# Attention steps spread over more half-slots, transposes of P earlier in SyncE's queue, one rotation product instead of two

## The reference

```
x = x + 0.5 * ffn(layernorm(x))
x = x + attn(layernorm(x))
x = x + 0.5 * ffn(layernorm(x))        # the same FFN weights again

ffn:  p = softmax(x @ router.T)        # 8 experts
      w = p where the cumulated sorted p stays within 0.9 (the first over it kept), else 0
      out = sum_e w[:, e] * ((silu(x @ gate_e.T) * (x @ up_e.T)) @ down_e.T)      # inner width 512
attn: q (16 heads of 16), k and v (4 heads of 16); bias; RMS norm and rotation of q and k; q * gain
      softmax(q k^T / 4 + causal mask) @ v, then @ Wo.T + bo
```

## Time and profile before

| | |
|---|---|
| median of three runs | 1158.7 us |
| the profiled execution | 1158.12 us |
| its span | 1156.4 us |
| TensorE busy | 1098.6 us, 95% |
| VectorE, ScalarE, GpSimd busy | 72%, 47%, 54% |
| mean DMA throughput | 48 GB/s |
| mean granted TensorE clock | 0.996 |

### The profile page before, as it was taken

One profiled execution on the slowest core, in us unless ns is written; L12 is line 12 of the kernel. 1 busy time (PEld: TensorE's weight loads), 2 busy tenths in 40 slices (PEclk: granted clock), 3 DMA queues, 4 the chain that ended last, 5 costly groups with the idle time before them and its releaser, 6 DMA issues.

```text
span 1156.4 us, 21016 instructions
## 1 busy us (share of the span) xinstructions
PE 1098.6 (95%) x7553; PEld 658.0 (57%) x7553; DVE 834.8 (72%) x1817; ACT 544.0 (47%) x1026; POOL 629.5 (54%) x657
## 2 busy tenths in 40 slices
PE   5899999998998998998998999999999999999998
PEld 2465555664564654664665655655655556556565
DVE  7878887666877877887887788787788765544443
ACT  4545544333644544654654555555555553333332
POOL 4544443446567557567567578577487453322322
PEclk9999999999999999999999999999999999999999
DMA  5411210000323223233232232333323321000000
GB/s 183 131 55 56 73 50 2 11 14 19 52 51 65 51 41 65 51 52 56 51 52 56 51 52 56 56 65 69 60 42 70 59 51 20 5 19 1 1 2 19
DMA packets 157303, 55.86 MB, mean 48 GB/s; under 512 B 149392, under 2 KB 154000, under 8 KB 157200
## 3 DMA queue, kind: packets, MB, share of 16 engines
q1 hardware_dynamic: 157200, 54.51, 22.4%
HBM read 15.70 MB, written 2.10 MB: 15 GB/s over the span
## 4 chain that ended last, share of the span: by engine, by line
PE 55%; POOL 8%; issue 3%; DMA 3%; DVE 2%; SPq 1%; ACT 1%; DVEq 0%; POOLq 0%; ACTq 0%
PE YB L338 18%; PE G L319 16%; PE U L319 16%; DMA QKT<-room 3%; POOL RR L1032 2%; POOL HS L976 2%; PE S L442 1%; PE S L428 1%; POOL room L1058 1%; PE S L411 1%; SPq L1155 1%; POOL XF L989 1%; PE S L393 1%; POOL RA L1027 1%; DVE X L627 1%
## 5 line engine op out<-in xcount | busy, mean ns | idle before, releaser
L976 POOL TENSOR_TENSOR HS<-TS,HS 128x512 f16<-128x512 f32 x256 | 301.3, 1177 | 402.6 <-ACT HS L491 402.0
L338 PE MATMUL YB<-W,HS 128*128 128x256 f16 x3036 | 377.3, 274 | 20.8 <-DVE X L627 16.9
L319 PE MATMUL G<-XS,W 128*128 128x512 f16 x1536 | 376.3, 381 | 1.7 <-ACT XS L516 1.7
L319 PE MATMUL U<-XS,W 128*128 128x512 f16 x1536 | 373.7, 379 | 1.0 <-DVE W L712 1.0
L338 PEld LDWEIGHTS YB<-W,HS 128*128 128x128 f16 x3036 | 289.9, 98 | 95.1 <-DVE X L627 25.5
L491 ACT ACTIVATE HS<-TS 128x512 f16<-128x512 f32 x256 | 161.3, 630 | 337.9 <-DVE TS L611 336.0
L606 DVE SCALAR_TENSOR_TENSOR TS<-TS,G 128x512 f32<-128x512 f32 x256 | 174.9, 683 | 191.0 <-ACT TS L484 190.7
L484 ACT ACTIVATE TS<-G,TSC 128x512 f32<-128x512 f32 x256 | 175.5, 685 | 180.9 <-PE G L319 176.8
L319 PEld LDWEIGHTS U<-XS,W 128*128 128x128 f16 x1536 | 150.3, 98 | 182.9 <-DVE W L712 1.5
L319 PEld LDWEIGHTS G<-XS,W 128*128 128x128 f16 x1536 | 150.0, 98 | 130.8 <-issue 2.6
L611 DVE SCALAR_TENSOR_TENSOR TS<-TS,U 128x512 f32<-128x512 f32 x256 | 176.0, 687 | 28.4 <-DVE TS L606 1.8
(11 more groups left out here) (160 smaller groups left out, 748.5 us busy)
## 6 DMA issues: line engine op xcount, KB each, us to landing
room<-in_gate SPq DMA_DIRECT2D x4, 512.0 KB, 3.5
room<-in_up SPq DMA_DIRECT2D x4, 512.0 KB, 3.4
room<-in_down SPq DMA_DIRECT2D x4, 512.0 KB, 4.3
QKT<-in_gate SPq DMA_DIRECT2D x4, 512.0 KB, 3.5
QKT<-in_up SPq DMA_DIRECT2D x4, 512.0 KB, 4.0
QKT<-in_down SPq DMA_DIRECT2D x4, 512.0 KB, 4.7
out_y<-X SPq DMA_DIRECT2D x16, 128.0 KB, 1.8
X<-in_x SPq DMA_DIRECT2D x3, 512.0 KB, 6.1
```

The source lines that it names most:

```text
L319: mm = eng.matmul(bank[:, :], W[:, e, wl, jj, kk * I + m * P:kk * I + (m + 1) * P], flat(XS16[:, b % 2, xl, kk, :, :], 'cq'), start=q == 0 ...
L338: mm = eng.matmul(out, HS[:, j % 2, hl, kk, m * P:(m + 1) * P], W[:, e, wl, 2, kk * D:(kk + 1) * D], start=kk + hl + wl == 0, stop=kk == K ...
L976: eng.tensor_tensor(HS[:, j % 2, 1, m, :], TS[:, k % 3, :], HS[:, j % 2, 0, m, :], ALU.subtract).then_inc(L['g_lo'].sem, 1)
```

## The change

Only places in the queues, one wait list and one VectorE product change. All shapes, matmuls and DMAs stay. Rounds 3 and 4 of a batch move from r = 20 and 26 to 18 and 27 (the others stay), the projection moves one slot later, so does most of what follows it; even and odd tiles' rounds get offsets of their own.

```diff
-ROUND = [FIRST + 2 + PER * i for i in range(NR)]
+ROUND_AT = (2, 8, 14, 18, 27, 32)
+ROUND = [FIRST + BATCH * (i // PER) + ROUND_AT[i % PER] for i in range(NR)]
...
-FTP_SOON, FTP_LATER, FTP_LAST, ROUTE_LATER = ((66, 68), (62, 64), (30, 51), 67)
+FTP_SOON, FTP_LATER, FTP_LAST, ROUTE_LATER = ((64, 64), (61, 62), (32, 49), 67)
...
-A_STEP = {'ax': 3, 'xl': 3, 'bo': 6}
-Q_STEP = {'rb1': 2, 'sq': 2, 'rb0': 2, 'rr': 3, 'r': 4, 'qn': 5, 'v': 5, 'qh': 6, 'ql': 6, 't': 7}
-I_STEP = {'ma': 1, 'mb': 2, 'ea': 2, 'eb': 3, 'ha': 3, 'hb': 4, 'la': 4, 'lb': 5, 't': 6, 'pv': 8, 'o': 9}
-R_STEP = {'r1': 1, 'ex': 1, 'r2': 1, 'r2b': 3, 'rank': 3, 'r3': 5}
+A_STEP = {'xn': 2, 'ax': 3, 'xl': 4, 't': 2, 'bo': 7}
+Q_STEP = {'qb': 1, 'rb': 1, 'sq': 1, 'ra': 2, 'ss': 2, 'rr': 4, 'r': 5, 'qn': 5, 'v': 7, 'qh': 6, 'ql': 7, 't': 6}
+EVEN_STEP = {'ma': 1, 'mb': 2, 'ea': 3, 'eb': 3, 'ha': 5, 'hb': 5, 'la': 4, 'lb': 4, 't': 2, 'pv': 8, 'o': 9}
+ODD_STEP = {'ma': 1, 'mb': 2, 'ea': 2, 'eb': 3, 'ha': 2, 'hb': 5, 'la': 3, 'lb': 4, 't': 3, 'pv': 8, 'o': 9}
+AT = {c: [ROUND[i] + (EVEN_STEP if i % PER < 2 else ODD_STEP)[c] for i in range(NR)] for c in EVEN_STEP}
+R_STEP = {'r1': 1, 'ex': 2, 'r2': 2, 'r2b': 3, 'rank': 4, 'r3': 5}
...
-O_STEP = {'ot': 2, 'mm': 2, 'ad': 3}
+O_STEP = {'ot': 1, 'mm': 2, 'ad': 3}
...
-ATP, QKVP, OUTP = (by_tile(-17, -5), by_tile(-12, 0), by_tile(18, 42))
-ATT = [s - 4 for s in ATP]
+ATT, QKVP, OUTP = (by_tile(-24, -12), by_tile(-11, 1), by_tile(18, 42))
...
-TILE = [s - 4 - (f % 2 == 0 and f >= 3 * BT) for f, s in enumerate(FTP)]
+TILE_AT = (-5, -4)
+TILE = [s + (TILE_AT[f % 2] if f >= NT else -4) - (f % 2 == 0 and f >= 3 * BT) for f, s in enumerate(FTP)]
...
-        def dve_rb(eng, t, a):
+        def dve_rb(eng, t):
...
-            eng.tensor_tensor(RB[:, :, a, :], q4[:, :, 1 - a, :], (SIN, NSIN)[a][:, t % 2, :].unsqueeze(1).broadcast_to([P, QK, HD // 2]), ALU.mult).then_inc(L['v_rb'].sem, 1)
+            eng.tensor_tensor(RB[:, :, :, :], q4[:, :, ::-1, :], SIGN[:, t % 2, :, :].unsqueeze(1).broadcast_to([P, QK, 2, HD // 2]), ALU.mult).then_inc(L['v_rb'].sem, 1)
...
         def sp_slot(eng, s):
-            for i in due(ROUND, s, I_STEP['t']):
+            for i in due(AT['t'], s):
                 sp_pt(eng, i)
-            for t in due(ATP, s):
+            for t in due(ATT, s, A_STEP['t']):
                 sp_atp(eng, t)
```

More of the change, by code:

```diff
@@ L169, in build @@
         GM, GE, GR, NESC = (sb(c, [P, 1], F32) for c in ('GM', 'GE', 'GR', 'NESC'))
-        COS, SIN, NSIN = (sb(c, [P, 2, HD // 2], F32) for c in ('COS', 'SIN', 'NSIN'))
+        COS, SIN = (sb(c, [P, 2, HD // 2], F32) for c in ('COS', 'SIN'))
+        SIGN = sb('SIGN', [P, 2, 2, HD // 2], F32)
         ident = sb('ident', [P, P], F32)
@@ L217, in build @@
                 ('v_fst', 'stats'), ('v_fag', 'aggr'), ('v_fep', 'eps'), ('v_fx', 'xn'), ('v_ls', 'ls mx sub'), ('v_rp', 'sum rc p eq gt'), ('v_wt', 'cum wt'), ('v_wb', 'wtc'), ('v_wc', 'wc'),
-                ('v_al', 'stats aggr eps'), ('v_ax', 'xn'), ('v_qb', 'qb'), ('v_ss', 'ss ms'), ('v_rb', 'rb1 rb0 r'), ('v_qn', 'qn'), ('v_ql', 'qlo klo'), ('v_mp', 'xa a xb b'), ('v_pv', 'rc rd ob'), ('v_op', 'ad'),
+                ('v_al', 'stats aggr eps'), ('v_ax', 'xn'), ('v_qb', 'qb'), ('v_ss', 'ss ms'), ('v_rb', 'rb r'), ('v_qn', 'qn'), ('v_ql', 'qlo klo'), ('v_mp', 'xa a xb b'), ('v_pv', 'rc rd ob'), ('v_op', 'ad'),
                 ('g_lo', 'lo'), ('g_w', 'lo2'), ('g_frs', 'rs'), ('g_fl', 'xl'), ('g_rk', 'eq b bp'), ('g_ars', 'rs'), ('g_al', 'xl'), ('g_bo', 'bo'), ('g_sq', 'sq'), ('g_rr', 'rr sg'), ('g_ra', 'ra'), ('g_v', 'v1 r1 v2 r2 v3'), ('g_pl', 'a b'), ('g_rw', 'b1 r1 b2 r2 b3')]:
@@ L297, in s2_read @@
         def s2_read(eng, s):
-            eng.wait_ge(*L['v_pv'].at(before(ROUND, s, I_STEP['pv']), 'rd'))
+            eng.wait_ge(*L['v_pv'].at(before(AT['pv'], s), 'rd'))
             eng.wait_ge(*L['v_qb'].at(before(QKVP, s), 'qb'))
@@ L459, in pe_slot @@
                 pe_scores(eng, i, s)
-            for i in due(ROUND, s, I_STEP['pv']):
+            for i in due(AT['pv'], s):
                 pe_pv(eng, i, s)
@@ L586, in act_slot @@
             for h in range(2):
-                for i in due(ROUND, s, I_STEP['e' + 'ab'[h]]):
+                for i in due(AT['e' + 'ab'[h]], s):
                     act_exp(eng, i, h)
             for h in range(2):
-                for i in due(ROUND, s, I_STEP['h' + 'ab'[h]]):
+                for i in due(AT['h' + 'ab'[h]], s):
                     act_ph(eng, i, h)
@@ L812, in dve_ss @@
             eng.tensor_scalar(MS[:, :], SS[:, :], 1.0 / HD, RMS_EPS, ALU.mult, ALU.add).then_inc(L['v_ss'].sem, 1)
-        def dve_rb(eng, t, a):
+        def dve_rb(eng, t):
             eng.wait_ge(*L['v_qb'].at(t, 'qb'))
             q4 = QKV[:, 0:QW].rearrange('p (h a c) -> p h a c', a=2, c=HD // 2)
-            eng.tensor_tensor(RB[:, :, a, :], q4[:, :, 1 - a, :], (SIN, NSIN)[a][:, t % 2, :].unsqueeze(1).broadcast_to([P, QK, HD // 2]), ALU.mult).then_inc(L['v_rb'].sem, 1)
+            eng.tensor_tensor(RB[:, :, :, :], q4[:, :, ::-1, :], SIGN[:, t % 2, :, :].unsqueeze(1).broadcast_to([P, QK, 2, HD // 2]), ALU.mult).then_inc(L['v_rb'].sem, 1)
         def dve_r(eng, t):
-            eng.wait_ge(*L['v_rb'].at(t, 'rb0'))
+            eng.wait_ge(*L['v_rb'].at(t, 'rb'))
             eng.wait_ge(*L['g_ra'].at(t, 'ra'))
@@ L846, in dve_max @@
                 eng.wait_ge(s_i2, 2)
-                eng.wait_ge(s_ag, 7)
+                eng.wait_ge(s_ag, 8)
             if t % 2 == 0:
@@ L880, in dve_constants @@
             eng.tensor_reduce(GM[:, :], GN[:, :], AX.X, ALU.max, apply_absolute_value=True).then_inc(lane, 1)
-            eng.tensor_scalar(NSIN[:, :, :], SIN[:, :, :], -1.0, None, ALU.mult).then_inc(lane, 1)
-            eng.wait_ge(lane, 2)
+            eng.tensor_scalar(SIGN[:, :, 0, :], SIN[:, :, :], 1.0, None, ALU.mult).then_inc(lane, 1)
+            eng.tensor_scalar(SIGN[:, :, 1, :], SIN[:, :, :], -1.0, None, ALU.mult).then_inc(lane, 1)
+            eng.wait_ge(lane, 3)
             eng.tensor_scalar(GM[:, :], GM[:, :], 1e-30, None, ALU.max).then_inc(lane, 1)
-            eng.wait_ge(lane, 3)
+            eng.wait_ge(lane, 4)
             eng.tensor_scalar(GE[:, :].bitcast(I32), GM[:, :].bitcast(I32), 2139095040, None, ALU.bitwise_and).then_inc(lane, 1)
-            eng.wait_ge(lane, 4)
+            eng.wait_ge(lane, 5)
             eng.reciprocal(GR[:, :], GE[:, :]).then_inc(lane, 1)
             eng.tensor_scalar(NESC[:, :], GE[:, :], -(float(HD) ** (-0.5)), None, ALU.mult).then_inc(lane, 1)
-            eng.wait_ge(lane, 6)
+            eng.wait_ge(lane, 7)
             eng.tensor_scalar(GF[:, :], GN[:, :], GR[:, 0:1], None, ALU.mult).then_inc(lane, 1)
@@ L901, in dve_slot @@
             for h in range(2):
-                for i in due(ROUND, s, I_STEP['m' + 'ab'[h]]):
+                for i in due(AT['m' + 'ab'[h]], s):
                     dve_max(eng, i, h)
-            for i in due(ROUND, s, I_STEP['o']):
+            for i in due(AT['o'], s):
                 dve_pv(eng, i)
-            for t in due(QKVP, s, 1):
+            for t in due(QKVP, s, Q_STEP['qb']):
                 dve_qb(eng, t)
@@ L911, in dve_slot @@
                 dve_a_stats(eng, t)
-            for t in due(ATT, s, 1):
+            for t in due(ATT, s, A_STEP['xn']):
                 dve_a_xn(eng, t)
[L914 to L917, removed]
+            for t in due(QKVP, s, Q_STEP['rb']):
+                dve_rb(eng, t)
+            for t in due(QKVP, s, Q_STEP['ss']):
                 dve_ss(eng, t)
@@ L1023, in pool_ra @@
         def pool_ra(eng, t):
+            eng.wait_ge(*L['v_qb'].at(t, 'qb'))
             eng.wait_ge(*L['v_qn'].at(t - 1, 'qn'))
@@ L1085, in pool_slot @@
             for h in range(2):
-                for i in due(ROUND, s, I_STEP['l' + 'ab'[h]]):
+                for i in due(AT['l' + 'ab'[h]], s):
                     pool_pl(eng, i, h)
@@ L1089, in pool_slot @@
                 pool_sq(eng, t)
+            for t in due(QKVP, s, Q_STEP['ra']):
                 pool_ra(eng, t)
```

## The result

The changed kernel takes 1116.9 us (median of four runs, 1116.35 to 1117.56) against 1158.8: a ratio of 0.9637, 95% interval 0.9623 to 0.9651. That is 41.9 us less; I had forecast 31 less, with a lower end of 1118. The direction and the places were right, the size was not, and the experiments show that two of my steps were wrong in a way that the total hides. Where a difference to the changed kernel is given as a range, it is against 1117.6 and against 1116.9.

What follows compares the result with a forecast made beforehand. TensorE, busy for 95% of the span, was taken as the bound: 17.0 (P) + 12 (X) + 3.2 (lo) + 5.1 (clock) won, 6 given back, net 31.3 off 1158.1, so 1127 us, range 1118 to 1143.

Steps and rivals of the forecast that it cites:

- The residue of 6 us: Waits on TensorE expected to stay or come: 4 us for round 4's P, 2 us for lo.
- the reachable sum: Most the change could win on TensorE: 34.2 us of waits plus 5.1 us of lower clock, 39.3 us.
- all of X: Waits of y for VectorE's add into X: 14.0 us reachable, 12 taken as gone, bounds 8 and 14.
- the rest of the moves at zero: `ot`, `bo`, router steps, `pool_ra`, FFN tiles: work moved within engines' idle time, zero, bounds 2 lost and 1 won.
- all 17.0 us before the product with V: TensorE's waits for P's transposes, put down to queueing on SyncE: 17.0 us won by placing P ahead.
- 3.2 for lo: TensorE's waits for GpSimd's lo: 3.2 us, to go with the late y.
- three stretches of 3.4 us at the lower clock: TensorE at half speed behind waits of 2.7 us or more: 5.1 us won, bounds 0 and 5.1.
- the lo of r = 34: On GpSimd behind round 4's low part and V's parts: 0.5 us late in four batches, 2 us, bounds 0 and 8.
- its own bounds: Whole forecast with residues 0 to 16 and X 8 to 14: 1120 to 1138 us.
- The queue explains the wait to the last tenth.: Round 4's P: SyncE issues its transpose 1.84 us after the low parts end; TensorE waited 1.83 us.
- GpSimd's lack of room: Rival: GpSimd's queue has 13.0 us of work in 12.0; 12 to 18 us more given back, 1141 us, chance 0.15.
- All of it goes: Rival: `qn` on VectorE isn't blocked by a lo, the 6 us don't come; 1119 to 1121 us, chance 0.12.

Runs made afterwards that it cites:

- a_rest_old: Changed kernel with the steps of the router, the second FFN's layernorm and transposes, and `ot` back where they were: 1124.9 us.
- b_both: Kernel before with P's transposes sooner in SyncE's queue and `qn` behind the add into X, none of the other moves: 1146.0 us.
- b_qn_later: Kernel before with only `qn` moved behind the add into X of its slot: 1168.9 us, ratio 1.009.
- b_p_v_qn: Kernel before with P's transposes sooner, V's parts two slots later on GpSimd and `qn` behind the add into X: 1133.6 us, ratio 0.978.

## Why the prediction was right and wrong

Two steps of the prediction failed. The residue of 6 us was a mis-sized term: no such wait came. And the reachable sum itself, 39.3 us, was too small, since it took each wait from the end of a TensorE row: 23 waits were longer than listed, by 3.7 us together. Even without any residue and with all of X my sum ends at 1118.8, above the 1116.4 of the profiled run. A third step, the rest of the moves at zero, was wrong too, but it is no separate term of the waits: what these moves bring was counted among the waits for X and lo.

*Which waits go.* Right: all 17.0 us before the product with V, 11.4 of those for X (I took 12), 3.2 for lo, and three stretches of 3.4 us at the lower clock, 5.1 us.

*The residue (4 + 2 us).* Wrong, the largest single part of the miss. For P the working gave a slack of 0.5 to 1.4 us, and I priced 0.5 us of wait all the same; the batch shown has 0.9, and no batch waits. A reckoned slack above nothing was charged as a cost. The 2 us were for the lo of r = 34, reckoned 0.5 us late. That count began at the worst end of the low parts, T + 3.2, took V's parts at 2.0 us and had them done at T + 7.1. In the trace the low parts end at T + 2.4, V's parts take 1.6 us and are done at T + 5.8, and this lo ends 1.0 us before it is wanted.

*The length of a wait.* Too short by about 0.16 us each. Before, the U ahead of round 4's product has six matmuls that start 0.216 us apart, 1.30 in all, while its row shows 1.46:

```profile
784.88 1.46 PE L319 MATMUL U<-XS,W 128*128 128x512 f16 x6
```

The row's end is modelled, and the listed wait counts only from there. The product could have started at 784.88 + 1.30 = 786.18; it lost 1.99 us, not 1.83. In the changed kernel, without a wait, the product starts 1.31 us after a y whose row shows 1.47. The listed waits for X, P and lo went from 30 to 7; over 23 of them this is 3.7 us, and it is most of why steady batches fell below what I had read. The Trainium skill says it too, in Perfetto Trace Analysis (section Tensor Engine Instruction): the end is an estimate worked out from the instruction's size and an SBUF delay. The rows here agree. I had even added the 0.16 into TensorE's being ready.

*The start.* G of chunk 16 starts at 85.5 us in the changed kernel's profile and at 87.3 before. 0.4 of these 1.8 us is the y that waits for X at 53 us, 1.3 in place of 1.7; it follows the routers' steps, since `a_rest_old` has 1.7 again, and is part of the 11.4. The other 1.4 us lie ahead of it and differ from run to run: this G starts between 85.5 and 87.1 in the traces of the changed kernel and its variants with the new routers' steps. That part is no effect of the change.

With the measured sizes the sum closes on the 41.8 us between the two profiled spans: 31.3 + 6 (residue) - 0.6 (X) + 3.7 (ends) + 1.4 (start) = 41.8.

One sum of the prediction is off as well: its own bounds, taken together, give 1118.8 to 1140.8, not 1120 to 1138.

*"The queue explains the wait to the last tenth."* True of one batch and wrong as a cause. The order alone leaves 5.3 us of waits for P; in the steady batch shown TensorE had itself been held for 1.7 us at y, and without that hold P would have been late by GpSimd's queue (`b_both` waits 2.0 us there). The waits at y and at P are links of one chain from the 3.5 us power on, not two terms. The three moves that I had priced (P ahead, `qn` behind the add, and V's parts, which I had counted on GpSimd but given no gain) end at 1133.6.

*"The rest: zero."* Wrong: 7.3 us for router, FFN and `ot` places, 2 to 3 each for the moved rounds, the rounds' offsets and the merged product. Taken back one by one they add up to 14.0 us of the 16.0 between 1133.6 and 1117.6, or 16.1 of the 16.7 down to 1116.9. Such a sum of single moves is only a guide, as these moves aren't additive either, and the places of the layernorm of x, of the projection and of the power, all moved, were not tried alone. My rows had no wait that named these steps, since a wait is put down to the last link (the add into X), and what stood ahead of the add isn't in that row.

So the total came within 10 us by offsetting errors, which is partly luck: the moves that I had reasoned about bring less than I gave them, and others that I took as nothing bring the rest. Of the rivals, GpSimd's lack of room was the most telling; it was the kernel before's state, not the changed one's. "All of it goes" (1119 to 1121) came nearest, but not by its mechanism: `qn` still took 1.37 us beside a lo, at the median of the 16 tiles, and the residue stayed away all the same.

## What to carry to other kernels

In a schedule by hand where every engine has a queue, the waits on the bounding engine are one chain: removing one link alone can gain part of what was counted (P ahead, 14.6 of 20.4 us) or lose 11 us (`qn` later), so follow the late queue back to its longest instruction (here 3.5 us on GpSimd) and make room behind it before valuing any single move. A slack that comes out positive is not a cost, and the true length of a TensorE wait is counted from the start of the last matmul plus its pitch (the time between two starts). Steps that no wait names can still be what stands ahead of the instruction that is named.

## What the hardware showed

- GpSimd's power over 128x20 took 3.54 us, as long as three lo over 128x512. Beside it VectorE's sum of two SBUF operands took 0.48 us in both batches shown, while `qn`, started 0.13 us behind a lo, took 1.37. In the changed kernel 1.37 is its median; before, it was 0.50, and 1.37 the longest.
- A reversed two-step dimension in an operand needn't cost anything: the product over 320 columns took 0.49 us at its fastest, as the sum over 320 did (0.48). Its median is 1.01, beside GpSimd's squares; why, no run here shows.
- In the changed kernel, whose longest wait in a batch is 1.5 us, the granted clock stayed at the upper level (2.4 GHz) in all eight batches. Before, it fell to 1.2 GHz for 3.4 us behind waits of 2.73, 2.75 and 3.55 us and not behind 2.52 and 2.53. The length of the wait alone doesn't decide: it fell behind 2.50 us in `a_rest_old` and not behind 3.56 us in `b_qn_later` (at 709.8) or 2.88 in `b_both` (at 360.1).
- In 14 of the 17 traces it fell in the start as well, for 3.4 us from about 25 us on (6.8 in `b_p_v_qn`), behind waits of 1.3 us at most since 10 us. That is 1.7 us of lost time, as much as many of the differences measured here.
